# First layer's attention: the values of four key chunks at a time from group 3 on, with seven buffers for the weights

## Chip, cores and metric

One NeuronCore of a Trainium2 chip runs the whole program in one launch. The metric is the device time in microseconds (us) of that core; it is given as the median of several executions.

## What is computed

Two layers over an input `x` of 2 batches x 128 positions x 256 features. The change lies in the first step of the first layer, a cross attention with 16 heads of 16 features over 2048 keys per batch, in which keys and values are both the context:

```python
scores = jnp.einsum('bhqd,bhkd->bhqk', qh, kh) / math.sqrt(hd)
qi = jnp.arange(Sq)[:, None] + (Sk - Sq)
ki = jnp.arange(Sk)[None, :]
causal = ki <= qi
scores = jnp.where(causal[None, None], scores, jnp.asarray(MASKED_BIAS, scores.dtype))
attn = jax.nn.softmax(scores, axis=-1)
out = jnp.einsum('bhqk,bhkd->bhqd', attn, vh)
...
x = x + _L0_xattn_ref(_layernorm(x, axis=-1), ctx_2048, ctx_2048)
x = x + _L0_attn_ref(_layernorm(x, axis=-1), L0_attn_A_log, L0_attn_D, L0_attn_W_xproj)
x = x + _L0_ffn_ref(...)
```

The second step, `_L0_attn_ref`, is a state space scan: step sizes from a projection and a softplus, a decay `exp(dt * A)` and an input `dt * B * x` for each of 16 states, a scan over the 128 positions, and a sum over the states with `C`. After it come a low-rank mixture of experts, and in the second layer another cross attention, a local attention and a feed-forward mixture. Those later parts are not touched.

## The kernel before

Every engine has its own instruction list, written out by hand in Python loops; engines meet only through counting semaphores, and each list is carried out in order.

**Groups.** The 2 x 16 heads are cut into eight groups of four heads, `g` = 0 to 7 (four of batch 0, then four of batch 1). A group goes over its 2048 keys in 16 chunks of 128, `c` = 0 to 15; the text numbers chunks through as n = 16 g + c. Keys are stored as bfloat16 parts in `kS[g % 3]`.

**Three streams on TensorE.** For group g the loop (L1047 on) goes over pairs of chunks, k = 0 to 7, c = 2 k:

- `scores_shifted(g, c)` (L889, with a masking matmul L888 in the last chunk): four matmuls of one chunk's scores with the maxima subtracted, into one of two PSUM banks `score_b[n % 2]`. It waits for the exponential of chunk n - 2 (`exp_done`).
- `values(g, c)` (L902): four products with the values, 128x32 tiles in float32, two passes each, so 8 matmul records a chunk; `pv_done` counts chunks. In the pair k the chunks c - 2 and c - 1 are taken.
- `scores_for_max` (L858, with L860 to L862 where the mask lies): sixteen parts a group, which give the scores of the *next* group for its row maxima; `MAX_AT` sets how many follow each pair. Two parts fill one of two double banks; VectorE reduces it (L1647, piece 0 to 7). `max_to_rows(g + 1)` (L872) closes the group and waits for that group's maxima (`nm_done`, L1653 to L1658 on VectorE).

At k = 1 `outputs_to_rows(g - 1)` (L910, L911) transposes the finished group.

**ScalarE** takes the exponential of each chunk (L665) from `score_b` into a weight buffer `pT[n % 3]`, after waiting for the values of chunk n - 3. Between exponentials it does the steps of its `beside` table, keyed (group, chunk): the copy of the outputs (L644 at c = 2, L655 at c = 4), the softplus (L585, L588, at (5, 0) and (5, 1), the second with a load of another activation table), the decay's exponentials `decay_exp` (L600, at (6, 2) and (6, 6)) and sixteen copies `bc_copy` (L595).

**The scan of batch 0 runs in the same stretch.** After group 3 VectorE normalises batch 0 (L1390 to L1396, after piece 2 of group 5) and gives the layer norm; TensorE projects (L921, L930); VectorE makes the input (`step_and_input`, L1406, L1408) and splits the projected maps (`split_maps`, L1418 to L1422). TensorE then spreads 32 rows of B and C over the partitions in 16 steps, `spread` (L945) at `SPREAD_AT`, each of which waits for the copy of the step before. GpSimd makes the decay's exponents (L422, twice) and the inputs (L414, twice), VectorE scans (L1439, after piece 3 of group 7) and multiplies by C (`read_states`, L1445, after piece 6 of group 7, once all sixteen copies are there). GpSimd's list has, after the copy of group 6's values (L433), `decay_exponent(0)`, `decay_exponent(1)` and `state_input(0, 0)`, then the copy of group 7's values and `state_input(0, 1)`. The decay lies where the key parts of batch 1 lay, so its exponents wait until the keys of group 7 have been fetched as well as for `dtx_done`; the inputs wait for eight of the sixteen copies:

```python
pool.wait_ge(S("kS_in1"), 16 * REP * 3)
...
pool.wait_ge(S("bc_sb"), (8, 20)[b])
```

**SyncE** fetches keys and values. For group g from 3 on:

```python
sp.wait_ge(S("pv_done"), NCH * (g - 2))
values_in(g - 1)
```

followed by twelve transfers into `kS[g % 3]` (L287). For group 7 that is a wait for the values of chunk 79, the last of group 4.

## Time and profile before

| | |
|---|---|
| median of 3 runs | 515.19 us (515.15 to 516.58) |
| profiled execution, its own time | 514.26 us |
| its span | 512.0 us, 8986 instructions |
| PE (TensorE) busy | 425.1 us, 83% |
| weight loads busy | 311.0 us, 61% |
| DVE (VectorE) busy | 345.8 us, 68% |
| ACT (ScalarE) busy | 269.4 us, 53% |
| POOL (GpSimd) busy | 121.7 us, 24% |
| chain that ended last, by engine | PE 58%, DVE 23%, ACT 8%, issue 6% |
| L902, values of the chunks | 1024 matmuls, 45.9 us |
| L889, shifted scores | 512 matmuls, 51.0 us |
| L1439, scan | 12.0 us for the two of batch 0 |

The span is the time between the first and the last instruction in the records; the execution's own time is 2.3 us more. Busy times of engines overlap, so they don't add up to the span, and matmuls are pipelined: a record starts when the matmul enters and ends when its last result is out, so several are open at once. The eight groups take the span from 38 us to 198 us.

### The profile page before, as it was taken

The page shows a single profiled execution, that of the slowest core. Times are in us where ns is not written, and L with a number is a line of the kernel's source. Part 1 is how long each engine was busy: PE and PEld are TensorE (multiplying, and loading weights), DVE is VectorE, ACT ScalarE, POOL GpSimd, SP SyncE. Part 2 cuts the span into 40 slices and gives each one's busy share as a digit, 9 for nine tenths or more (in the row PEclk, how much of TensorE's full clock was granted, in tenths as well). Part 3 has the DMA queues.
Part 4 walks back from the last instruction along what each step waited for, and adds up shares of the span by engine and source line. Part 5 has one row for each costly group of instructions (what it writes and reads, how often), then busy time and mean ns, then how long its engine had stood idle before and what let it go on. Part 6 is the DMA issues. An engine that isn't in the chain of part 4 may idle for free.

```text
span 512.0 us, 8986 instructions
## 1 busy us (share of the span) xinstructions
PE 425.1 (83%) x3584; PEld 311.0 (61%) x3584; DVE 345.8 (68%) x544; ACT 269.4 (53%) x579; POOL 121.7 (24%) x78
## 2 busy tenths in 40 slices
PE   0269889988875985694989998997789799999997
PEld 0116556656553773534843473445679699999996
DVE  3797667676569935699565565684562589778772
ACT  4305697766585452540322442457784076777762
POOL 3010545000274000280003235250300213333300
PEclk9999899998797798678999999999799979999999
DMA  6598176652511082000920000005800197540000
GB/s 217 141 291 214 28 187 166 165 133 52 150 48 32 3 299 68 25 0 1 397 97 1 1 0 3 0 0 193 300 1 2 43 360 246 173 165 1 2 2 20
DMA packets 24329, 54.11 MB, mean 106 GB/s; under 512 B 5113, under 2 KB 13529, under 8 KB 20954
## 3 DMA queue, kind: packets, MB, share of 16 engines
q1 hardware_dynamic: 24288, 53.54, 33.4%
q8 instruction: 28, 0.46, 0.4%
q14 instruction: 13, 0.11, 0.1%
HBM read 40.65 MB, written 0.26 MB: 80 GB/s over the span
## 4 chain that ended last, share of the span: by engine, by line
PE 58%; DVE 23%; ACT 8%; issue 6%; DMA 2%; POOL 2%; SPq 0%; ACTq 0%; DVEq 0%; POOLq 0%
PE ps L1268 17%; PE ps L1089 8%; PE ps L902 5%; PE ps L889 4%; PE ps L858 4%; DVE mx L1647 4%; DVE reg_b L1439 3%; DVE reg_a L1439 2%; ACT reg_b L665 2%; PE ps L1233 2%; PE ps L1223 2%; PE ps L1222 2%; PE ps L997 2%; PE ps L1016 1%; DVE reg_b L1430 1%
## 5 line engine op out<-in xcount | busy, mean ns | idle before, releaser
L1647 DVE TENSOR_REDUCE mx<-ps 128x1 f32<-128x1024 f32 x64 | 77.0, 1221 | 40.4 <-PE ps L858 28.3
L665 ACT ACTIVATE reg_b<-ps 128x512 f32<-128x512 f32 x128 | 75.4, 599 | 39.9 <-PE ps L889 20.8
L889 PE MATMUL ps<-qreg,reg_b 98*128 98x128 bf16 x512 | 51.0, 235 | 6.1 <-ACT reg_b L665 4.7
L889 PEld LDWEIGHTS ps<-qreg,reg_b 98*128 98x128 bf16 x512 | 38.3, 106 | 18.6 <-ACT reg_b L665 8.8
L1268 PE MATMUL ps<-part_a 128*128 128x256 f32 x384 | 48.2, 283 | 0.4 <-DVE part_a L1792 0.4
L386 POOL TENSOR_TENSOR rstd<-ve,cf 128x1 f32<-128x1 f32 x12 | 6.8, 563 | 172.3 <-DVE ve L1341 172.3
L858 PE MATMUL ps<-reg_b,qreg 96*128 96x512 bf16 x96 | 36.3, 448 | 13.7 <-DMA reg_b<-reg_b 7.6
L1089 PE MATMUL ps<-reg_b,xT 128*128 128x512 f32 x96 | 47.6, 618 | 0.0
L1268 PEld LDWEIGHTS ps<-part_a 128*128 128x128 f32 x384 | 46.9, 192 | 0.6 <-DVE part_a L1792 0.6
L902 PE MATMUL ps<-reg_b 128*32 128x128 f32 x1024 | 45.9, 299 | 0.0
L800 ACT ACTIVATE reg_a<-ps,b 128x256 f32<-128x256 f32 x64 | 30.2, 472 | 24.0 <-PE ps L1268 24.0
L1792 DVE TENSOR_TENSOR part_a<-reg_a,part_a 128x256 fp32r<-128x256 f32 x64 | 26.1, 431 | 18.8 <-ACT part_a L803 18.8
L1268 PE MATMUL ps<-part_a,part_b 128*128 128x256 f32 x288 | 38.2, 293 | 0.6 <-DVE part_a L1792 0.6
L1268 PEld LDWEIGHTS ps<-part_a,part_b 128*128 128x128 f32 x288 | 37.1, 202 | 0.9 <-DVE part_a L1792 0.8
L674 ACT COPY reg_a<-ps 128x512 f32<-128x512 f32 x24 | 14.0, 587 | 44.7 <-PE ps L1089 44.7
L902 PEld LDWEIGHTS ps<-reg_b 128*32 128x32 f32 x1024 | 26.8, 117 | 7.3 <-issue 1.9
L498 POOL CAST part_b<-reg_b 128x1024 fp32r<-128x1024 f32 (+1 forms) x9 | 16.3, 1827 | 46.6 <-PE ps L1268 34.0
L803 ACT CAST part_a<-reg_a 128x256 fp32r<-128x256 f32 x64 | 26.0, 407 | 2.0
L1089 PEld LDWEIGHTS ps<-reg_b,xT 128*128 128x128 f32 x96 | 16.3, 189 | 16.7 <-issue 16.7
L858 PEld LDWEIGHTS ps<-reg_b,qreg 96*128 96x128 bf16 x96 | 8.2, 103 | 26.4 <-DVE mx L1647 12.0
L460 POOL TENSOR_TENSOR qreg<-qreg,cf 128x16 f32<-128x16 f32 x4 | 13.4, 3356 | 35.2 <-DVE qreg L1587 35.2
L1739 DVE TENSOR_TENSOR part_a<-reg_b,part_a 128x1024 fp32r<-128x1024 f32 (+1 forms) x12 | 20.8, 1744 | 0.8 <-ACT part_a L811 0.8
(279 smaller groups left out, 869.8 us busy)
## 6 DMA issues: line engine op xcount, KB each, us to landing
reg_b<-in_w SPq DMA_DIRECT2D x16, 512.0 KB, 7.1
reg_b<-in_w SPq DMA_DIRECT2D x8, 1024.0 KB, 7.0
reg_b<-reg_b SPq DMA_DIRECT2D x56, 128.0 KB, 3.7
reg_b<-in_w_qkv SPq DMA_DIRECT2D x3, 2048.0 KB, 13.4
reg_b<-reg_a SPq DMA_DIRECT2D x40, 128.0 KB, 3.6
reg_a<-in_ctxK SPq DMA_DIRECT2D x4, 1024.0 KB, 6.9
reg_a<-in_ctx SPq DMA_DIRECT2D x8, 512.0 KB, 5.1
reg_a<-in_ctxT SPq DMA_DIRECT2D x2, 2048.0 KB, 9.7
```

The costliest lines, as they stand in the source:

```text
L665: sc.activation(pT[n % 3], score_b[n % 2], ACT.Exp).then_inc(S("exp_done"), 1)
L800: sc.activation(hid[layer][:, m, :], ps[:, 2 + m, 0:NB * P], ACT.Gelu, bias=(b1, b2)[layer][:, e, m:m + 1]).then_inc(S(f"h{layer + 1}_sb"), 1)
L803: sc.copy(hid_high[layer][:, m, :], hid[layer][:, m, :]).then_inc(S(f"h{layer + 1}_high"), 1)
L858: mm = pe.matmul(score_a[m % 2][:, i, :], q, k, start=True, stop=True)
L889: mm = pe.matmul(cols, kS[g % 3][0:SROWS, c // 8, j, P * (c % 8):P * (c % 8 + 1)], qT[b][0:SROWS, HPG * hg + j, :], start=not last, stop=True)
L902: mm = pe.matmul(ps[VW * j:VW * (j + 1), 7, 0:P], va[g % 2][:, c, j, :], pT[n % 3][:, P * j:P * (j + 1)], start=c == 0, stop=c == NCH - 1)
L1089: mm = pe.matmul(bank(b, n % 2), xT[b][:, i, :], w_qkv[:, j, i, 512 * n:512 * (n + 1)], start=False, stop=i == KD - 1)
L1268: mm = pe.matmul(out, left[u], right[v], start=(i, u, v) == (0, 0, 0), stop=(i, u, v) == (len(terms) - 1, 0, 1))
L1439: link(ve.tensor_tensor_scan(state[b][:, h].rearrange("p n l -> p (n l)"), decay[b][:, h].rearrange("p n l -> p (n l)"), state[b][:, h].re ...
L1647: ve.reduce_max(mx[:, piece // 2, piece % 2:piece % 2 + 1], score_a[m % 2].rearrange("p i k -> p (i k)"), X_AXIS).then_inc(S("max_done"), 1)
L1739: ve.tensor_tensor(low[e % 2][i], raw[e % RAW][i], high[e % 2][i], ALU.subtract).then_inc(S("w_low"), 1)
L1792: ve.tensor_tensor(hid_low[layer][:, m, :], hid[layer][:, m, :], hid_high[layer][:, m, :], ALU.subtract).then_inc(S(f"h{layer + 1}_low"), 1)
```

## The change

From group 3 on (`QUADS = 3`) TensorE no longer takes the values of two chunks in every pair, but of four in every second one: at odd k the chunks n - 6 to n - 3 of the pair that begins with chunk n. Seven weight buffers instead of three make room for it (four more at `reg_b` 16384 to 17920), and ScalarE waits for the values of chunk n - 7. The outputs of the group before are transposed at k = 2 instead of k = 1, and ScalarE copies them at c = 4 and c = 6 instead of 2 and 4. `state_maps` moves from (5, 4) to (5, 7), the sixteen spreads move to other chunks, and on VectorE `split_maps` comes after `step_and_input` and one more piece.

```diff
-SPREAD_AT = [(5, c) for c in range(8, 15)] + [(6, c) for c in (0, 1, *range(4, 11))]
+SPREAD_AT = [(5, c) for c in range(9, 15)] + [(6, c) for c in (0, 1, 2, *range(7, 14))]
+QUADS = 3
...
-        pT = [reg_b[:, 24576 + 512 * i:24576 + 512 * (i + 1)] for i in range(3)]
+        pT = [reg_b[:, a:a + 512] for a in (24576, 25088, 25600, 16384, 16896, 17408, 17920)]
+
+        def weight_buffer(n):
+
+            first = NCH * QUADS
+            return pT[n % 3] if n < first else pT[(n - first + 3) % 7]
...
-                    if g >= 1 and c == 2:
+                    if g >= 1 and c == (2 if g < QUADS else 4):
                         unnormalised(g - 1)
-                    if g >= 1 and c == 4:
+                    if g >= 1 and c == (4 if g < QUADS else 6):
                         sc.wait_ge(S("oT_ready"), g)
...
-                    if n >= 3:
+                    if 3 <= n < NCH * QUADS:
                         sc.wait_ge(S("pv_done"), n - 2)
-                    sc.activation(pT[n % 3], score_b[n % 2], ACT.Exp).then_inc(S("exp_done"), 1)
+                    elif n >= NCH * QUADS + 4:
+                        sc.wait_ge(S("pv_done"), max(n - 6, NCH * QUADS))
+                    sc.activation(weight_buffer(n), score_b[n % 2], ACT.Exp).then_inc(S("exp_done"), 1)
...
-                      (5, 4): [(misc_read, "o_all", 5), (state_maps, 0)], (6, 4): [(misc_read, "o_all", 6)],
+                      (5, 7): [(misc_read, "o_all", 5), (state_maps, 0)], (6, 7): [(misc_read, "o_all", 6)],
...
+            def chunks_at(g, k):
+
+                n = NCH * g + 2 * k
+                if g < QUADS:
+                    return range(max(n - 2, 0), n)
+                if k % 2 == 0:
+                    return ()
+                return range(max(n - 6, NCH * QUADS - 2), n - 2)
...
-                    if k > 0:
-                        values(g, c - 2)
-                        values(g, c - 1)
-                    elif g > 0:
-                        values(g - 1, NCH - 2)
-                        values(g - 1, NCH - 1)
-                    if k == 1 and g >= 1:
+                    for chunk in chunks_at(g, k):
+                        values(*divmod(chunk, NCH))
+                    if k == (1 if g < QUADS else 2) and g >= 1:
...
-            values(NG - 1, NCH - 2)
-            values(NG - 1, NCH - 1)
+            for c in range(NCH - 4, NCH):
+                values(NG - 1, c)
...
-                      (5, 4): [(ln_apply, 1, 0)], (5, 8): [(step_magnitude, 0)], (6, 2): [(split_maps, 0)],
-                      (6, 3): [(step_and_input, 0)], (7, 3): [(scan, 0, 0)], (7, 6): [(read_states, 0, 0)]}
+                      (5, 4): [(ln_apply, 1, 0)], (5, 8): [(step_magnitude, 0)], (6, 3): [(step_and_input, 0)],
+                      (6, 4): [(split_maps, 0)], (7, 3): [(scan, 0, 0)], (7, 6): [(read_states, 0, 0)]}
```

How the lists now stand, at three places. (Line numbers of the changed kernel are larger: L897 is the old L889, L910 the old L902, L866 the old L858; on ScalarE L673 is the old L665, L601 the old L595, L606 the old L600.)

TensorE at the start of group 5, from the scores of chunks 80 and 81 to those of chunk 83 and the values behind them. `exp_done` is ScalarE's count of exponentials, `max_done` VectorE's of reduced pieces. Before:

```order
L889 MATMUL ps<-qreg,reg_b 128x128 [waits exp_done,ones_in,nm_rows]
L889 MATMUL ps<-qreg,reg_b 128x128 x3
L889 MATMUL ps<-qreg,reg_b 128x128 [waits exp_done]
L889 MATMUL ps<-qreg,reg_b 128x128 x3
L902 MATMUL ps<-reg_b 32x128 [waits exp_done]
L902 MATMUL ps<-reg_b 32x128 x3
L902 MATMUL ps<-reg_b 32x128 [waits exp_done]
L902 MATMUL ps<-reg_b 32x128 x3
L858 MATMUL ps<-reg_b,qreg 128x512 [waits max_done]
```

Now:

```order
L897 MATMUL ps<-qreg,reg_b 128x128 [waits exp_done,ones_in,nm_rows]
L897 MATMUL ps<-qreg,reg_b 128x128 x3
L897 MATMUL ps<-qreg,reg_b 128x128 [waits exp_done]
L897 MATMUL ps<-qreg,reg_b 128x128 x3
L866 MATMUL ps<-reg_b,qreg 128x512 [waits max_done]
L868 MATMUL ps<-reg_b,qreg 128x384
L869 MATMUL ps<-reg_b,qreg 128x128
L870 MATMUL ps<-cb 128x128
L897 MATMUL ps<-qreg,reg_b 128x128 [waits exp_done]
L897 MATMUL ps<-qreg,reg_b 128x128 x3
L897 MATMUL ps<-qreg,reg_b 128x128 [waits exp_done]
L897 MATMUL ps<-qreg,reg_b 128x128 x3
```

Right behind the last of these stand the values of chunks 76 to 79. The values of chunks 78 and 79 stood behind the scores of chunk 81; they now stand behind the scores of chunk 83.

ScalarE at the start of group 6, from the maxima's rows to the second copy after them; L595 is a copy of spread rows, L600 the exponential of the decay. Before:

```order
L571 COPY qreg<-ps 2x512
L665 ACTIVATE reg_b<-ps 128x512 x2
L595 COPY reg_b<-ps 128x256
L665 ACTIVATE reg_b<-ps 128x512
L644 COPY o_sb<-ps 128x128
L600 ACTIVATE reg_a<-reg_a 128x2048
```

Now:

```order
L577 COPY qreg<-ps 2x512
L673 ACTIVATE reg_b<-ps 128x512 x2
L601 COPY reg_b<-ps 128x256
L673 ACTIVATE reg_b<-ps 128x512
L606 ACTIVATE reg_a<-reg_a 128x2048
L601 COPY reg_b<-ps 128x256
```

The copy ahead of the decay's exponential was the eighth of the sixteen and is now the seventh; the eighth follows the exponential.

ScalarE at the end of group 6, the last copy and what follows it up to the next group's rows. Before:

```order
L665 ACTIVATE reg_b<-ps 128x512
L595 COPY reg_b<-ps 128x256
L665 ACTIVATE reg_b<-ps 128x512 x4
L571 COPY qreg<-ps 2x512
L665 ACTIVATE reg_b<-ps 128x512 x3
```

Now:

```order
L673 ACTIVATE reg_b<-ps 128x512
L601 COPY reg_b<-ps 128x256
L673 ACTIVATE reg_b<-ps 128x512
L577 COPY qreg<-ps 2x512
L673 ACTIVATE reg_b<-ps 128x512 x5
```

The sixteenth copy stood ahead of chunk 11's exponential and now stands ahead of chunk 14's.

## Rows read from the trace of the kernel before

**Rows 1.** Groups 3 and 6: us; busy PE, PEld, DVE, ACT, POOL; clock; DMA share, GB/s.
```profile
91.20:105.70 14.50, 14.01 (x229) 9.50 (x228) 10.34 (x12) 10.70 (x21) 1.04 (x1) 1.00 0.57 147
...
148.30:174.40 26.10, 19.46 (x244) 12.73 (x242) 22.19 (x19) 16.25 (x31) 10.09 (x3) 0.74 0.15 39
```

**Rows 2.** Timeline of TensorE, group 3: start us, us, engine, line, operation.
```profile
95.28 0.61 PE L889 MATMUL ps<-qreg,reg_b 98*128 98x128 bf16 x8
95.82 0.64 PE L902 MATMUL ps<-reg_b 128*32 128x128 f32 x16
96.40 0.34 PE L860 MATMUL ps<-reg_b,qreg 96*128 96x384 bf16 x1
```

**Rows 3.** One line's own view, L902: ns of one, min/median/max.
```profile
L902 PE MATMUL ps<-reg_b x1024: 269/273/423, 40.9 to 197.4; 128*32 128x128 f32 x171
```

**Rows 4.** Timeline of all engines, chunks 80 to 84: bracket is idle before, releaser.
```profile
126.11 0.33 SPq L261 DMA_DIRECT2D reg_a<-in_ctx  x1
...
127.71 1.28 ACT L665 ACT_TABLE_LOAD   x1
129.00 0.60 ACT L665 ACTIVATE reg_b<-ps 128x512 f32<-128x512 f32 x1
...
129.65 0.61 PE L889 MATMUL ps<-qreg,reg_b 98*128 98x128 bf16 x4 [2.78 <-ACT reg_b L665]
130.19 1.08 PE L902 MATMUL ps<-reg_b 128*32 128x128 f32 x16
```

**Rows 5.** The same timeline, SyncE's last two transfers of group 7's keys.
```profile
133.36 1.22 SPq L287 DMA_DIRECT2D reg_b<-reg_b  x2
```

**Rows 6.** DMA issues, 126 to 140 us: median us to landing of those two.
```profile
reg_b<-reg_b SPq DMA_DIRECT2D x2, 128.0 KB, 3.2
```

**Rows 7.** Timeline, 138 to 172 us: GpSimd's exponents and VectorE's maxima.
```profile
139.10 7.17 POOL L422 TENSOR_TENSOR reg_a<-tmpb,ea 128x2048 f32<-128x2048 f32 x2 [5.65 <-DVE tmp L1408]
...
144.36 1.94 DVE L1653 TENSOR_TENSOR m<-mx 128x4 f32<-128x4 f32 x1
...
147.07 0.33 PE L872 MATMUL ps<-cb,nm 128*2 128x128 bf16 x3 [0.62 <-ACT reg_b L595]
...
171.49 0.16 DVE L1653 TENSOR_TENSOR m<-mx 128x4 f32<-128x4 f32 x1
```

**Rows 8.** Timeline, 149 to 173 us: inputs, decay and the two scans.
```profile
149.69 4.55 POOL L414 TENSOR_TENSOR reg_a<-tmp,reg_b 128x2048 f32<-128x2048 f32 x1 [3.41 <-ACT reg_b L595]
...
150.26 1.92 ACT L600 ACTIVATE reg_a<-reg_a 128x2048 f32<-128x2048 f32 x1
...
154.28 1.04 POOL L433 COPY reg_b<-reg_a 128x1024 f32<-128x1024 f32 x1
...
155.28 4.54 POOL L414 TENSOR_TENSOR reg_a<-tmp,reg_b 128x2048 f32<-128x2048 f32 x1
...
156.55 7.55 DVE L1439 TENSOR_TENSOR_SCAN reg_a<-reg_a 128x2048 f32<-128x2048 f32 x1
...
172.80 4.42 DVE L1439 TENSOR_TENSOR_SCAN reg_a<-reg_a 128x2048 f32<-128x2048 f32 x1
```

**Rows 9.** Timeline, 214 to 234 us: VectorE and GpSimd side by side, batch 1.
```profile
215.50 8.82 DVE L1430 TENSOR_TENSOR reg_b<-tmpb,ea 128x2048 f32<-128x2048 f32 x2
215.60 13.11 POOL L414 TENSOR_TENSOR reg_b<-tmp,reg_b 128x2048 f32<-128x2048 f32 x2 [0.46 <-ACT reg_b L595]
```

**Rows 10.** Timeline after the first scan: spreads, copies, values and C.
```profile
165.42 1.04 PE L858 MATMUL ps<-reg_b,qreg 96*128 96x512 bf16 x2 [3.14 <-DVE mx L1647]
...
167.95 1.08 PE L902 MATMUL ps<-reg_b 128*32 128x128 f32 x16
168.03 2.29 DVE L1445 TENSOR_TENSOR reg_a<-reg_a,reg_b 128x2048 f32<-128x2048 f32 x1 [0.32 <-ACT reg_b L595]
```

**Rows 11.** Chain that ended last, in order of time: start us, us, what.
```profile
177.26 2.30 DVE reg_a L1445
...
189.48 0.44 PE ps L824 x2
```

More of the change, by code:

```diff
@@ L901, in values @@
                 for j in range(HPG):
-                    mm = pe.matmul(ps[VW * j:VW * (j + 1), 7, 0:P], va[g % 2][:, c, j, :], pT[n % 3][:, P * j:P * (j + 1)],
+                    mm = pe.matmul(ps[VW * j:VW * (j + 1), 7, 0:P], va[g % 2][:, c, j, :], weight_buffer(n)[:, P * j:P * (j + 1)],
                                    start=c == 0, stop=c == NCH - 1)
@@ L1031, in _ @@
                 beside.setdefault(at, []).append((spread, 0, i))
-            read_before_rows = {2: ("qT_sb", 4), 3: ("qT_sb", 6), 5: ("z_sb", 1), 6: ("bc_sb", 7), 7: ("bc_sb", 16)}
+            read_before_rows = {2: ("qT_sb", 4), 3: ("qT_sb", 6), 5: ("z_sb", 1), 6: ("bc_sb", 6), 7: ("bc_sb", 16)}
             read_before_outputs = {5: ("bc_sb", 9)}
```

## Prediction

> **What bounds the kernel now.** I began with the chain that ended last: it goes through the attention at every group, so what moves the end of group 7 moves the end of the program. Next the busy times by stretch [rows 1]. They show two kinds of group. In group 3 TensorE is busy 14.01 of 14.50 us: it is the bound. Group 6 lasts 26.10 us with TensorE busy 19.46, ScalarE 16.25 and VectorE 22.19, so there something else decides. The timeline says what: scores part 12 is held 3.14 us behind a VectorE reduction [rows 10], the reduction behind a scan of 7.55 us, and the scan had to wait for GpSimd's first input, which ends at 154.24 [rows 8]. From that scan on the chain stays on VectorE (three reductions, the product with C, one more reduction, the maxima, the second scan, the second product that ends at 179.56) and reaches the next layer norm's transposes at 189.48 [rows 11]. So two chains meet in groups 5 and 6, and the question is what the change does to the one through GpSimd and VectorE.
>
> **What is gained.** Eight matmuls of scores start at 95.28 and the values at 95.82 [rows 2]. One of these matmuls lasts 0.22, so the eight with 0.61 are (0.61 - 0.22) / 7 = 0.056 us apart and would need 0.45; 0.09 is extra. The sixteen of the values with 0.64, one of 0.27 [rows 3], are 0.025 apart and need 0.40, but the next matmul comes after 0.58: 0.18 extra. One batch of values costs 0.27 us for going over to the narrow tiles and back. From group 3 to the end there are 41 batches, and afterwards 21: 20 x 0.27 = 5.4 us of TensorE's time, the most that the edit can take away.
>
> **Why little of it arrives.** In a pair without values TensorE needs 8 x 0.056 = 0.45 plus two or three parts of 0.22: about 1 us. ScalarE needs 2 x 0.60 [rows 4] for the pair, about 1.3 with its waits, and with only two score banks the second scores of the next pair wait for it: 0.3 to 0.5 us in each double pair, against the 0.27 saved. Extra weight buffers don't help; they relieve the values, not the banks. Outputs of a group are copied two chunks later, so normalising batch 0 starts about 1 us later. I put groups 3 and 4 at 0 to +1 us, and take +0.5.
>
> **First cost: group 7's keys are fetched later.** SyncE sends them off once chunk 79's values are done, at 126.11 [rows 4]. The order above puts these values behind the scores of chunk 83, which wait for chunk 81's exponential. That stands behind the softplus with two loads of a table, the one listed of 1.28 us and its like before it; it ends at 129.60, and TensorE goes on at 129.65 after 2.78 us of idling. Then 0.54 of scores, and four chunks of values where the rows have two for 130.19 to 131.21, at half clock: 2.04 instead of 1.02. That is 132.2, with the 0.5 from above 132.7, call it +6.6. The transfers keep their 10.9 us (last one issued at 133.97 [rows 5], 3.2 to landing [rows 6], so 137.2): 143.8. GpSimd's exponents, which began at 139.10 when VectorE had their input [rows 7], had 1.9 us to spare; now the keys come last, and the two run 143.8 to 151.0: **+4.7 us**.
>
> **Second cost: the maxima of group 6 fall into them.** VectorE's first small operation at 144.36 took 1.94 us and ended with GpSimd's at 146.3; the same one takes 0.16 with GpSimd idle [rows 7]. Four such follow each other, and the last has two SBUF inputs like the first. In the new order they come at about 146 (the split and the input in the other order cost nothing, the third piece comes at the same time), in the middle of 143.8 to 151.0. The first gets in between the two exponents at best, the last then waits for the end of the second: maxima at about 151.4, rows at 151.5 instead of 147.07, **+4.4 us**. TensorE stands still about 3 us for it, and I expect its clock at the lower of its two levels (1.2 instead of 2.4 GHz) afterwards, as after the 2.78 us before 129.65, where sixteen matmuls of values took 1.08 instead of 0.64 [rows 2, 4]. The Trainium skill's page "SBUF — State Buffer", section "SBUF: two separate sides", says that a GpSimd instruction and a VectorE one with two SBUF inputs or in a two-port mode lock each other out for the whole instruction. By that rule the maxima end as I have them; were the port shared by bandwidth, they would end 3 us earlier.
>
> **Third cost: the eighth copy.** From the rows to GpSimd's first input it took 149.69 - 147.07 = 2.6 us. Added ahead of the eighth copy: the decay's exponential, 1.92 [rows 8]; one more chunk with its spread and copy, about 0.8 (165.42 to 167.95 holds two parts of 0.4 and two such rounds [rows 10]); two more chunks of values, 0.4; and at the lower clock about 0.6 more. 6.3 us, so the input starts at 157.8 and ends at 162.35, +8.1.
>
> **What comes back.** The first scan takes 7.55 us, the second 4.42 [rows 8]: the first waited until 159.8 for GpSimd's second input. In batch 1 both engines took turns: two of VectorE in 8.82 and two of GpSimd in 13.11, about the sum of both alone, 4 x 2.3 and 4.5 [rows 9]. In the new order the scan waits behind the copy of the values (1.04) and then, if turns are taken, goes before the second input: 163.5 to 167.9. Before, it ended at 164.1: **+3.8 us** of the 8.1 is left.
>
> **Fourth cost: the sixteenth copy.** The product with C waits for it: 168.03 - 164.10 = 3.9 us after the scan [rows 10]. TensorE is again held at part 12 until 1.3 us after the scan, and from there now has two parts, a spread round and scores (the 2.5 of the same rows), four chunks of values at low clock (2.1), two parts (0.9), then two chunks each with a spread that waits for the copy before (2 x 0.9), and ScalarE the exponential of chunk 13 and the copy (1.0). 1.3 + 2.5 + 2.1 + 0.9 + 1.8 + 1.0 = 9.6 at the low clock, 7.5 at the high one. I take 9.0: **+5.1 us**. The last piece, the maxima, the second scan all stand behind that product.
>
> **Sum.** 3.8 + 5.1 = 8.9, and about 0.3 in group 7, where the scores of the last chunks wait for exponentials: **+9.2 us**. VectorE's chain from the product with C to 189.48 is unchanged, and after group 7 nothing is. The profiled execution's own 514.26 becomes 523.5; the median of the runs is 0.9 above it, so I say **524.4 us**. The sum's own bounds are +5.5 (high clock throughout, two of the 3 us of collision spared) and +13.5 (the scan loses the turn and waits for the second input too, 4.5 us).
>
> **Rivals.**
>
> - *No late exponents.* If the values of chunk 79 are not held up that much, or GpSimd's exponents slip past the maxima, the first two costs shrink to about 1 us. For it: 1.9 us to spare. Against: the table loads are in the way whatever else changes. Then the input starts 4 us late, the scan at 159.4 once the values are copied and ends at 163.8, -0.3; the sixteenth copy still costs 3.6 to 5.1. Sum +4.5: **519.7 us**. Chance 0.22.
> - *Faster.* The saved switches arrive: TensorE reaches chunk 13 of group 6 so early that the sixteenth copy is no later than 3.9 us after the scan. This decides at 3.9 us against the 7.5 that I work out, so the spreads would have to be done before the scan, which the hold at part 12 prevents; it needs the scan itself held up less by GpSimd than I think. Price: 2.7 (half of 5.4) to 5.4 off, say **511.5 us**. Chance 0.12.
> - *Nothing moves.* Gain in groups 3 and 4 of up to 2 us against a short delay: 515, chance 0.05.
> - That the change doesn't halve the batches can be left out: the order shows them in fours.
> - *More than the sum.* Scan behind the second input and low clock: 528, taken into the main case's range.
>
> **How the numbers follow.** Main case 0.61, no late exponents 0.22, faster 0.12, nothing 0.05. A measurement of this kernel can tell about 0.3%, 1.5 us, from no change. So slower 0.83, same 0.05, faster 0.12. The range takes the main case and the first rival with their bounds, 517 to 529, and leaves out the two cases below and a little above.
>
> **What would show it.** Right, step by step: idle time of TensorE before chunk 83's scores; group 7's first transfer issued at 132 to 134; GpSimd's exponents starting at about 144 released by a transfer, not by VectorE; one of VectorE's four-column operations lasting over 1 us; TensorE's rows for group 6 at 151 or later; a first scan of about 5 us instead of 7.55; VectorE idle for over 3 us before the product with C, released by a copy. Wrong: a first transfer before 129, exponents starting by 140, or that product starting within 4 us of the scan.

## The result: slower by 3.4%, and the profile after

| | before | after |
|---|---|---|
| median | 515.17 us of 4 runs (513.49 to 516.58) | 529.50 us of 4 runs (528.03 to 530.94) |
| ratio, 95% interval | | 1.034 (1.029 to 1.039) |
| profiled execution, own time | 514.26 us | 530.94 us |
| span | 512.0 us | 528.8 us |

The ratio is the one on record, from fast executions of both kernels; the two medians above are 2.8% apart. The forecast was 524.4 us with a range of 517 to 529; the kernel took 529.5, half a microsecond outside. The sign and most steps of the mechanism were as forecast; the size was not, 14.3 us instead of 9.2, and one step, the start of the scan, was worked out wrongly.

From the page of the profile after, its span and its line on busy time:

```profile
span 528.8 us, 8982 instructions
...
PE 428.9 (81%) x3584; PEld 316.2 (60%) x3584; DVE 347.1 (66%) x544; ACT 267.8 (51%) x579; POOL 125.7 (24%) x78
```

No engine works much more than before (TensorE 428.9 us against 425.1, GpSimd 125.7 against 121.7). The 16.8 us of span are waits for the most part, and some low clock. To find them I measure one stretch in every kernel, from group 3's first scores to the end of group 7's last values. Busy times by stretch, before (columns as in [rows 1]); the windows are group 3, group 5 up to group 6's rows, and from there to the product with C:

```profile
91.20:105.60 14.40, 13.91 (x228) 9.46 (x227) 10.34 (x12) 10.60 (x21) 1.04 (x1) 1.00 0.57 148
...
124.60:147.00 22.40, 17.70 (x224) 11.67 (x222) 14.71 (x21) 14.99 (x29) 8.21 (x3) 0.85 0.37 95
147.00:168.00 21.00, 14.51 (x193) 9.38 (x197) 16.07 (x9) 14.06 (x26) 10.09 (x3) 0.81 0.19 48
```

After, cut at the same events:

```profile
92.40:106.80 14.40, 13.19 (x213) 9.20 (x212) 10.33 (x12) 10.51 (x21) 1.04 (x1) 1.00 0.55 148
...
127.00:152.50 25.50, 15.09 (x208) 10.46 (x207) 18.14 (x21) 14.07 (x27) 8.21 (x3) 0.86 0.33 84
152.50:181.50 29.00, 21.68 (x245) 14.88 (x245) 13.70 (x10) 16.10 (x31) 14.14 (x3) 0.71 0.14 34
```

Group 3 lasts 14.40 us in both, group 4 is 1.2 us longer (20.20 against 19.00, the gap between the first windows), group 5 3.1 (25.50 against 22.40), and the third window 8.0 (29.00 against 21.00), at a lower clock; the rest of the stretch, 30.6 after and 29.6 before, gives 1.0. The stretch is 106.4 us before and 119.7 after, **+13.3**. Of the other 3.5 us, 1.2 lie before group 3, where nothing was changed, and 2.3 after group 7. The second figure has no link to an edit: over all fourteen profiled kernels what follows group 7 took from 310.5 to 316.7 us, at random as far as I can see, and single executions of the kernel before took 509.0 to 517.2. So below, the stretch tells where time goes, and the ratio what it is worth.

### The profile page after: what moved, and what is told of

Same layout as the page of the kernel before. It is cut to its first block, busy times and chain, and to the rows that moved or that the text cites. A ratio compares the mean times of both kernels' runs of the same rounds, so it can differ in the third digit from the quotient of the medians.

```text
span 528.8 us, 8982 instructions
## 1 busy us (share of the span) xinstructions
PE 428.9 (81%) x3584; PEld 316.2 (60%) x3584; DVE 347.1 (66%) x544; ACT 267.8 (51%) x579; POOL 125.7 (24%) x78
## 4 chain that ended last, share of the span: by engine, by line
PE 59%; DVE 22%; ACT 8%; issue 7%; DMA 2%; POOL 1%; SPq 0%; ACTq 0%; DVEq 0%; POOLq 0%
PE ps L1281 17%; PE ps L1102 8%; PE ps L910 7%; PE ps L866 4%; PE ps L897 4%; DVE mx L1660 3%; DVE reg_b L1452 2%; ACT reg_b L673 2%; PE ps L1246 2%; DVE reg_a L1452 2%; PE ps L1235 1%; PE ps L1236 1%; PE ps L1005 1%; PE ps L1024 1%; DVE reg_b L1443 1%
## 5 line engine op out<-in xcount | busy, mean ns | idle before, releaser
L1660 DVE TENSOR_REDUCE mx<-ps 128x1 f32<-128x1024 f32 x64 | 76.8, 1221 | 47.2 <-PE ps L866 35.6
L673 ACT ACTIVATE reg_b<-ps 128x512 f32<-128x512 f32 x128 | 74.4, 598 | 42.1 <-PE ps L897 32.9
L897 PE MATMUL ps<-qreg,reg_b 98*128 98x128 bf16 x512 | 50.1, 234 | 7.7 <-ACT reg_b L673 6.6
L897 PEld LDWEIGHTS ps<-qreg,reg_b 98*128 98x128 bf16 x512 | 38.3, 106 | 20.3 <-ACT reg_b L673 10.4
L866 PE MATMUL ps<-reg_b,qreg 96*128 96x512 bf16 x96 | 37.3, 461 | 16.0 <-DVE mx L1660 8.2
L1102 PE MATMUL ps<-reg_b,xT 128*128 128x512 f32 x96 | 50.2, 647 | 0.0
L1281 PE MATMUL ps<-part_a 128*128 128x256 f32 x384 | 48.2, 283 | 0.4 <-DVE part_a L1805 0.4
L910 PE MATMUL ps<-reg_b 128*32 128x128 f32 x1024 | 44.7, 313 | 0.0
L1805 DVE TENSOR_TENSOR part_a<-reg_a,part_a 128x256 fp32r<-128x256 f32 x64 | 26.2, 435 | 18.3 <-ACT part_a L811 18.3
L910 PEld LDWEIGHTS ps<-reg_b 128*32 128x32 f32 x1024 | 30.5, 124 | 5.5 <-issue 1.5
L504 POOL CAST part_b<-reg_b 128x1024 fp32r<-128x1024 f32 (+1 forms) x9 | 16.5, 1847 | 47.9 <-PE ps L1281 34.0
L866 PEld LDWEIGHTS ps<-reg_b,qreg 96*128 96x128 bf16 x96 | 7.6, 103 | 29.9 <-DVE mx L1660 13.7
L439 POOL COPY reg_b<-reg_a 128x1024 f32<-128x1024 f32 x8 | 8.3, 1047 | 54.8 <-DMA reg_a<-in_ctx 33.1
## 6 DMA issues: line engine op xcount, KB each, us to landing
reg_b<-in_w SPq DMA_DIRECT2D x16, 512.0 KB, 7.5
reg_a<-in_ctx SPq DMA_DIRECT2D x8, 512.0 KB, 4.6
```

What stands on the lines that cost most here:

```text
L504: pool.tensor_copy(high[e % 2][i], raw[e % RAW][i]).then_inc(S(name), 1)
L673: sc.activation(weight_buffer(n), score_b[n % 2], ACT.Exp).then_inc(S("exp_done"), 1)
L866: mm = pe.matmul(score_a[m % 2][:, i, :], q, k, start=True, stop=True)
L897: mm = pe.matmul(cols, kS[g % 3][0:SROWS, c // 8, j, P * (c % 8):P * (c % 8 + 1)], qT[b][0:SROWS, HPG * hg + j, :], start=not last, stop=True)
L910: mm = pe.matmul(ps[VW * j:VW * (j + 1), 7, 0:P], va[g % 2][:, c, j, :], weight_buffer(n)[:, P * j:P * (j + 1)], start=c == 0, stop=c == N ...
L1102: mm = pe.matmul(bank(b, n % 2), xT[b][:, i, :], w_qkv[:, j, i, 512 * n:512 * (n + 1)], start=False, stop=i == KD - 1)
```

## The steps in the trace after

The timeline of all engines where chunk 79's values were forecast to be late; start us, us, engine, line, operation, in brackets the idle time before and its releaser:

```profile
129.80 1.28 ACT L673 ACT_TABLE_LOAD   x1
131.09 1.08 ACT L673 ACTIVATE reg_b<-ps 128x512 f32<-128x512 f32 x2
131.75 0.61 PE L897 MATMUL ps<-qreg,reg_b 98*128 98x128 bf16 x4 [3.24 <-ACT reg_b L673]
132.29 1.94 PE L910 MATMUL ps<-reg_b 128*32 128x128 f32 x32
134.28 0.33 SPq L267 DMA_DIRECT2D reg_a<-in_ctx  x1
```

TensorE idles 3.24 us before chunk 83's scores, the four chunks of values follow at the low clock, and SyncE's transfers for group 7 begin at 134.28 (the one listed is group 6's values, the keys follow). What that does to GpSimd's exponents and VectorE's maxima, and those to TensorE's rows for group 6:

```profile
144.73 7.17 POOL L428 TENSOR_TENSOR reg_a<-tmpb,ea 128x2048 f32<-128x2048 f32 x2 [4.73 <-DMA reg_b<-reg_b]
...
146.15 2.21 DVE L1666 TENSOR_TENSOR m<-mx 128x4 f32<-128x4 f32 x1
...
148.39 3.54 DVE L1668 TENSOR_SCALAR negm<-m,cf 128x4 f32<-128x4 f32 x1
...
151.96 0.17 DVE L1670 CAST nm<-negm 128x4 bf16<-128x4 f32 x1
...
152.44 0.48 PE L880 MATMUL ps<-cb,nm 128*2 128x128 bf16 x3 [4.53 <-issue]
```

The exponents are now released by a transfer. VectorE's first small operation ends at 148.36 with the first exponent, the second at 151.93 with the second. Then the first input, the scan and what holds it:

```profile
157.24 1.92 ACT L606 ACTIVATE reg_a<-reg_a 128x2048 f32<-128x2048 f32 x1
159.03 0.38 ACT L601 COPY reg_b<-ps 128x256 f32<-128x256 f32 x1
...
159.56 4.53 POOL L420 TENSOR_TENSOR reg_a<-tmp,reg_b 128x2048 f32<-128x2048 f32 x1 [7.66 <-ACT reg_b L601]
...
160.29 1.94 PE L910 MATMUL ps<-reg_b 128*32 128x128 f32 x32
...
162.28 0.33 SPq L267 DMA_DIRECT2D reg_a<-in_ctx  x1
...
165.44 0.62 PE L866 MATMUL ps<-reg_b,qreg 96*128 96x512 bf16 x1
...
165.68 1.22 DVE L1660 TENSOR_REDUCE mx<-ps 128x1 f32<-128x1024 f32 x1 [1.23 <-PE ps L870]
...
166.91 1.04 POOL L439 COPY reg_b<-reg_a 128x1024 f32<-128x1024 f32 x1 [2.82 <-DMA reg_a<-in_ctx]
166.98 5.25 DVE L1452 TENSOR_TENSOR_SCAN reg_a<-reg_a 128x2048 f32<-128x2048 f32 x1
167.91 8.62 POOL L420 TENSOR_TENSOR reg_a<-tmp,reg_b 128x2048 f32<-128x2048 f32 x1
```

The decay's exponential and then the eighth copy stand ahead of the input, as in the forecast. The input ends at 164.09, but the scan starts at 166.98: it stands in VectorE's list behind the reduction of piece 3, which waits until 165.68 for its parts. It stood behind that reduction in the kernel before as well, 2.3 us after the end of the input (154.24):

```profile
155.25 1.22 DVE L1647 TENSOR_REDUCE mx<-ps 128x1 f32<-128x1024 f32 x1 [0.51 <-PE ps L862]
```

One thing is new. SyncE fetches group 7's values (L267) only once the values of chunk 95 are done, and these are now in a batch of four one pair later: the transfer goes off at 162.28, 2.7 us after the first input has started, where before it went 0.1 us after it (149.77 against 149.69), and GpSimd's copy waits for it until 166.91. Before, the copy came right behind the first input, and the second input began 1.3 us ahead of the scan [rows 8]; now the scan is first.

And the product with C:

```profile
181.06 0.37 ACT L601 COPY reg_b<-ps 128x256 f32<-128x256 f32 x1
181.46 2.29 DVE L1458 TENSOR_TENSOR reg_a<-reg_a,reg_b 128x2048 f32<-128x2048 f32 x1 [5.62 <-ACT reg_b L601]
```

VectorE idles 5.62 us for the sixteenth copy, where it idled 0.32 [rows 10].

TensorE's clock in successive windows of this stretch (columns as in [rows 1]):

```profile
148.80:155.70 6.90, 3.27 (x41) 2.27 (x42) 3.46 (x3) 1.17 (x2) 3.10 (x1) 0.51 0.00 0
155.70:159.10 3.40, 1.59 (x20) 1.09 (x18) 2.36 (x2) 3.10 (x5) 0.00 (x0) 1.00 0.00 0
159.10:165.90 6.80, 6.34 (x57) 4.36 (x58) 1.44 (x2) 3.87 (x10) 4.53 (x1) 0.50 0.35 80
165.90:172.70 6.80, 3.26 (x58) 2.33 (x56) 6.73 (x4) 4.00 (x7) 5.79 (x2) 1.00 0.23 67
```

The clock goes back and forth between 2.4 GHz (1.00) and 1.2 GHz (0.50). It falls for the second time at 159.10, after TensorE has been busy 1.59 of 3.40 us, and this low window, in which it is busy 6.34 of 6.80 us, lies exactly on the work that the scan waits for.

## The experiments

Twelve more kernels were run. All times below but the ratio are of one profiled execution each, in us after the first scores of group 3 (stretch: end of group 7's last values). The ratio is the one on record, to the kernel before on the same chip, with its 95% interval; it can differ from the quotient of two medians by a few tenths of a per cent.

| kernel | GpSimd's exponents begin | rows of group 6 | first input | scan | product with C | rows of group 7 | stretch | ratio |
|---|---|---|---|---|---|---|---|---|
| before | 47.9 | 55.8 | 58.4 | 65.3 to 72.9 | 76.8 | 82.0 | 106.4 | 1 |
| after | 52.4 | 60.1 | 67.2 | 74.6 to 79.9 | 89.1 | 93.5 | 119.7 | 1.034 (1.029 to 1.039) |
| a1 | 48.3 | 64.4 | 70.7 | 75.3 to 79.8 | 88.7 | 93.1 | 119.4 | 1.030 (1.022 to 1.038) |
| a2 | 52.5 | 60.2 | 67.5 | 73.8 to 78.2 | 87.5 | 87.7 | 118.7 | 1.023 (1.012 to 1.033) |
| a3 | 52.3 | 60.3 | 66.1 | 71.4 to 75.9 | 84.7 | 89.1 | 115.4 | 1.017 (1.009 to 1.026) |
| b1 | 48.2 | 56.2 | 61.7 | 68.1 to 76.0 | 85.3 | 89.7 | 116.0 | 1.017 (1.009 to 1.025) |
| c1 | 49.8 | 58.6 | 64.2 | 70.4 to 74.9 | 84.1 | 88.5 | 115.7 | 1.019 (1.014 to 1.024) |
| c2 | 52.3 | 60.0 | 67.1 | 74.6 to 79.8 | 84.7 | 89.7 | 115.0 | 1.011 (1.004 to 1.017) |
| c3 | 48.9 | 58.8 | 62.7 | 68.0 to 72.4 | 77.3 | 82.5 | 107.7 | 1.001 (0.997 to 1.004) |
| d1 | 46.4 | 62.7 | 68.4 | 74.9 to 82.7 | 92.1 | 96.5 | 122.0 | 1.024 (1.019 to 1.029) |
| e1 | 47.7 | 55.7 | 58.3 | 65.2 to 69.6 | 74.3 | 79.8 | 105.3 | 1.000 (0.996 to 1.004) |
| e2 | 54.7 | 55.5 | 61.8 | 66.5 to 70.9 | 79.6 | 83.9 | 113.5 | 1.014 (1.006 to 1.022) |
| e3 | 49.7 | 58.5 | 62.4 | 67.7 to 72.1 | 81.5 | 81.6 | 112.1 | 1.016 (1.011 to 1.022) |
| e4 | 48.7 | 56.6 | 59.3 | 66.1 to 70.6 | 78.7 | 79.6 | 108.0 | 1.001 (0.998 to 1.005) |

**a1, the late values put back.** On the kernel after:

```diff
                 n = NCH * g + 2 * k
+                if g == 5 and k < 2:
+                    return range(n - 4, n) if k == 0 else ()
```

> The changed kernel, but the values of chunks 76 to 79 stand in pair 0 of group 5 and none in pair 1, so that the fetch of group 7's keys no longer stands behind the table loads. Theory (late keys, then GpSimd's exponents across the maxima): the first key transfer starts at about 128 us instead of 134.7, the exponents at about 140 released by VectorE's input or nearly so, no small VectorE operation is held, the rows of group 6 come 4 to 5 us earlier, and the time falls from 529.5 by about 5, to 523 to 526. Rival (the quads themselves cost the time, by the two score banks): 529 to 530, no change.

The keys came early and the exponents began at 48.3, yet the stretch got hardly shorter (119.4), and the median was 527.75 us, not 523 to 526. Here is why, on the timeline of a1:

```profile
137.91 0.22 DVE L1437 CAST bc_split<-bc_res 32x128 bf16<-32x128 f32 x1
...
138.09 7.17 POOL L428 TENSOR_TENSOR reg_a<-tmpb,ea 128x2048 f32<-128x2048 f32 x2 [4.30 <-DMA reg_b<-reg_b]
...
138.48 3.30 DVE L1437 CAST bc_split<-bc_res 32x128 bf16<-32x128 f32 x1
...
141.82 3.59 DVE L1436 TENSOR_TENSOR bc_res<-bc_res,bc_split 32x128 f32<-32x128 f32 x1
...
145.72 0.39 PE L953 MATMUL ps<-bc_split,cb 96*128 96x128 bf16 x2 [7.69 <-DVE bc_split L1437]
```

The change also put the splitting of the maps behind the input. So with early keys the exponents fall on the split instead of on the maxima: two operations of 0.22 and 0.28 us alone take 3.30 and 3.59, and TensorE idles 7.69 us before the first spread. The late keys had kept the split clear. Undoing them by themselves moves the collision and takes nothing away.

**c1, the keys early again and the split ahead of the input.** a1's edit, and (the split at (6, 3); in the kernel before it stood at (6, 2))

```diff
-(6, 3): [(step_and_input, 0)], (6, 4): [(split_maps, 0)],
+(6, 3): [(split_maps, 0), (step_and_input, 0)],
```

> The changed kernel with the values of chunks 76 to 79 in pair 0 of group 5, and VectorE's split of the maps ahead of the scan's input again. Moving the values alone brought the keys back (exponents at 138.1) and left the rows at 154.2, since the split then fell into GpSimd's exponents. Theory (lock between GpSimd and VectorE, on the maxima or on the split, whichever is behind): with both out of its way the split ends before the exponents begin, the first copy of spread rows comes at about 140 instead of 142.6 or 146.5, the rows of group 6 at 148 to 149, and from the first scores of group 3 to the last values it takes 116 instead of 119.7 us. Rival (the rows of group 6 are late by TensorE's own order): rows at 152 or later, 119.

Neither collision is left: every operation of split and maxima takes 0.17 to 0.29 us. The stretch falls by 4.0 us against the kernel after. So the exponents' fall on VectorE's small operations costs some 4 us, on the maxima (after) as on the split (a1), and moving the keys alone doesn't get rid of it. The 4.0 may understate it: group 6's rows still come 2.7 us later than in the kernel before (58.6), since split and input now stand together ahead of a reduction, and TensorE idles 3.54 us behind the reductions that follow.

**d1, the orders of the change with the values in twos.** On the kernel after:

```diff
-QUADS = 3
+QUADS = 8
...
-            for c in range(NCH - 4, NCH):
+            for c in range(NCH - 2, NCH):
```

> The changed kernel with the values in twos in all groups and three buffers; state maps, split and spreads stay at the changed kernel's places. Theory (side work): close to the kernel before with the spreads moved (115.9 us from group 3's first scores to the last values, 1.017 of the time before), so 116 to 118, and the quads make the other 2 to 4. Rival (the quads are all of it): 107 and 515.

The stretch is 122.0, 2.3 longer than with fours. The same collision as in a1 is there (casts of 2.18 and 3.21 us, first spread after 6.04 us of idling):

```profile
142.53 3.21 DVE L1435 CAST bc_split<-bc_res 32x128 bf16<-32x128 f32 x1
...
146.36 0.40 PE L953 MATMUL ps<-bc_split,cb 96*128 96x128 bf16 x2 [6.04 <-DVE bc_split L1435]
```

So the orders that came with the fours cost this much without them. The forecast of 116 to 118 was too low: it left out the collision, and the scan takes 7.8 us again. That the fours themselves cost nothing can't be read from this, as d1's collision and scan are other ones than those of the kernel after.

**e2, the exponents held until the maxima are through.** On the kernel after:

```diff
                 if g == 6:
+                    pool.wait_ge(S("nm_done"), 7)
                     decay_exponent(0)
```

> The changed kernel, with one wait more: GpSimd's exponents of the decay wait for the maxima of group 6. Theory (of the second cost: the maxima are held by the exponents): no small operation of VectorE is held, the rows of group 6 come 55 to 56 us after group 3's first scores instead of 60.1, the first input at 63 instead of 67.2, and the last values at 116 instead of 119.7. Rival (rows late by TensorE): rows at 59 or later.

```profile
144.02 0.16 DVE L1667 TENSOR_TENSOR m<-mx 128x4 f32<-128x4 f32 x1
...
144.68 0.17 DVE L1672 TENSOR_TENSOR nm<-negm,nm 128x4 bf16<-128x4 f32 x1
...
144.93 7.17 POOL L428 TENSOR_TENSOR reg_a<-tmpb,ea 128x2048 f32<-128x2048 f32 x2 [6.98 <-DVE nm L1672]
```

An added wait makes the kernel faster. The exponents start 2.3 us later, the four small operations are short, group 6's rows come at 55.5 instead of 60.1, and the stretch is 6.2 us shorter. This takes away the second cost alone, and one wait is enough for it. At the rows it is worth 4.6 us, as forecast; at the scan's start the gain is 8.1, and of that 6.2 reach the end.

**a3, copies ahead of whatever else ScalarE has beside a chunk.** On the kernel after; it puts the eighth copy ahead of the decay's exponential:

```diff
-                beside.setdefault((g, c + 1), []).append((bc_copy, 0, i))
+                beside.setdefault((g, c + 1), []).insert(0, (bc_copy, 0, i))
```

> The changed kernel, but ScalarE makes the eighth copy of spread rows ahead of the decay's exponential (1.92 us) at chunk 2 of group 6. Theory (the copy is held by the exponential, and with it GpSimd's input, the spread behind it and the values of chunks 92 to 95): the input starts 1.9 us earlier, the scan by about 2, the time falls by 2 to 527.5. Rival (other work hides it): 529 to 530.

The first input starts only 1.1 us earlier, but the scan 3.2 and the product 4.4, and the stretch is 4.3 shorter. The timeline of a3:

```profile
157.25 1.91 ACT L606 ACTIVATE reg_a<-reg_a 128x2048 f32<-128x2048 f32 x1
...
157.50 4.54 POOL L420 TENSOR_TENSOR reg_a<-tmp,reg_b 128x2048 f32<-128x2048 f32 x1 [6.60 <-ACT reg_b L601]
...
157.92 1.08 PE L910 MATMUL ps<-reg_b 128*32 128x128 f32 x32
...
161.52 1.23 DVE L1660 TENSOR_REDUCE mx<-ps 128x1 f32<-128x1024 f32 x1 [0.71 <-PE ps L870]
...
162.82 4.42 DVE L1452 TENSOR_TENSOR_SCAN reg_a<-reg_a 128x2048 f32<-128x2048 f32 x1
163.97 4.10 POOL L439 COPY reg_b<-reg_a 128x1024 f32<-128x1024 f32 x1 [1.93 <-DMA reg_a<-in_ctx]
```

Exponential and input now run together, the same 32 matmuls of values take 1.08 us instead of 1.94, and piece 3 is reduced 5.2 us after the input's start, instead of 7.3. Part of this is the clock; how much, no run separates. The last row shows the lock from the other side: GpSimd's copy, 1.04 us elsewhere, takes 4.10 under the scan.

**b1, the spreads alone, on the kernel before.**

```diff
-SPREAD_AT = [(5, c) for c in range(8, 15)] + [(6, c) for c in (0, 1, *range(4, 11))]
+SPREAD_AT = [(5, c) for c in range(9, 15)] + [(6, c) for c in (0, 1, 2, *range(7, 14))]
...
-6: ("bc_sb", 7)
+6: ("bc_sb", 6)
```

> The kernel before with one part of the change alone: the sixteen spreads at the changed kernel's places. Values stay in twos, buffers three. Theory (third and fourth cost are the spreads' places): the eighth copy comes after the decay's exponential and the sixteenth ahead of chunk 14's, the product with C starts 4 to 8 us later, time 519 to 523. Rival (the quads cost the time): 515 to 516.

```profile
150.98 4.52 POOL L414 TENSOR_TENSOR reg_a<-tmp,reg_b 128x2048 f32<-128x2048 f32 x1 [6.31 <-ACT reg_b L595]
...
157.40 7.86 DVE L1439 TENSOR_TENSOR_SCAN reg_a<-reg_a 128x2048 f32<-128x2048 f32 x1
...
174.61 2.29 DVE L1445 TENSOR_TENSOR reg_a<-reg_a,reg_b 128x2048 f32<-128x2048 f32 x1 [5.74 <-ACT reg_b L595]
```

The places of the sixteen spreads alone, with no fours and no late keys, cost 9.6 us of stretch and 1.7% of the time: 3.1 by the scan's end, where the eighth copy was late, and 5.4 more by the product, where the sixteenth was.

**c2, the last nine spreads drawn together.** On the kernel after; chunks 7, 8 and 9 take two each, so that the sixteenth is at chunk 10 again:

```diff
-SPREAD_AT = [(5, c) for c in range(9, 15)] + [(6, c) for c in (0, 1, 2, *range(7, 14))]
+SPREAD_AT = [(5, c) for c in range(9, 15)] + [(6, c) for c in (0, 1, 2, 7, 7, 8, 8, 9, 9, 10)]
```

> The changed kernel, but the spreads of group 6 behind chunk 2 stand two and two at chunks 7, 8 and 9 and one at 10, so that the sixteenth copy stands ahead of chunk 11's exponential as in the kernel before. Theory (the sixteenth copy holds VectorE): the product with C starts about 4 us after the first scan instead of 9.3, and from group 3's first scores to the last values it takes about 115 instead of 119.7 us. Rival (the copy is late because TensorE is, whatever its place): still over 8 us after the scan, 119.

```profile
164.66 5.27 DVE L1452 TENSOR_TENSOR_SCAN reg_a<-reg_a 128x2048 f32<-128x2048 f32 x1
...
174.78 2.29 DVE L1458 TENSOR_TENSOR reg_a<-reg_a,reg_b 128x2048 f32<-128x2048 f32 x1 [1.24 <-ACT reg_b L601]
```

Up to the scan's end nothing changes (79.8), then the product comes 4.9 us behind it instead of 9.2: -4.4, and -4.7 on the stretch. That is the fourth cost by itself.

**c3, four edits together and the fours kept.** c2, c1's two edits, and the eighth copy ahead of the decay's exponential:

```diff
+            beside[6, 2].insert(0, (bc_copy, 0, SPREAD_AT.index((6, 1))))
             for i, (g, c) in enumerate(SPREAD_AT):
+                if (g, c) != (6, 1):
```

> The changed kernel with all four: values of 76 to 79 earlier, split ahead of the input, eighth copy ahead of the decay's exponential, spreads in twos. The quads stay. Theory (the side work's places cost the time, the quads nothing): 105 to 108 us from group 3's first scores to the last values, against 106.4 in the kernel before, time 512 to 517, the kernel before within 1 %. Rival (the quads cost 4 us by the score banks): 110, time 519 to 521.

The stretch is 107.7 us, the ratio 1.001 (0.997 to 1.004) over ten runs: no difference from the kernel before. Of the 13.3 us 12.0 are gone, about the sum of what c1, c2 and a3 took away one by one (4.0 + 4.7 + 4.3 = 13.0). So the places of the side work account for nearly all of the loss.

What the fours are worth by themselves c3 doesn't tell, for it isn't the kernel before with fours put in. Its split stands at (6, 3) as in c1, and `state_maps` and the outputs' copies are where the change put them; group 6's rows come 3.0 us later than before. Against that its scan takes 4.42 us instead of 7.55, as the values' copy and the second input come late. Beside e1 below, which is the kernel before with a scan of 4.42, its stretch is 2.4 us longer.

**a2, e3: the product with C after the maxima of group 7.** In VectorE's list of the kernel after (a2) and of c3 (e3):

```diff
-(7, 6): [(read_states, 0, 0)]
+(7, 8): [(read_states, 0, 0)]
```

> The changed kernel, but VectorE's product with C stands behind the maxima of group 7 instead of ahead of their last piece. Theory (the sixteenth copy holds the maxima and with them group 7): rows of group 7 come 5 us or more earlier, the second scan still follows the product, the product itself stays bound by the copy at about 181; the time falls by 2 to 5. Rival (that copy costs nothing, VectorE's chain is the same in either order): 529 to 530.

> The kernel with quads and all four undone, and the product with C behind the maxima of group 7. In the changed kernel this brought the rows of group 7 forward by 5.8 us and the last values by 1.0. Theory (VectorE's chain through product, second scan and second product ends last, not TensorE's rows): rows of group 7 2 to 4 us earlier, last values within 1 us of 107.7. Rival (TensorE's group 7 ends last): last values 2 us or more earlier, 513 or less.

In a2 the rows of group 7 come 5.8 us earlier, the stretch is only 1.0 shorter: the chain of product, second scan and second product decides there, not the rows. For e3 I expected rows 2 to 4 us earlier and last values within 1 us of c3's, and both were wrong: the copy is hardly late in c3, so the product had only 1.2 us of waiting to give away. It moved 4.2 us back (81.5), the rows came 0.9 earlier, and the stretch is 4.4 longer.

**e1, e4: the lock in the kernel before.** GpSimd's second input waits for the piece of group 7 that follows the scan; e4 has the edit of a2 as well.

```diff
+                if (b, h) == (0, 1):
+                    pool.wait_ge(S("max_done"), 8 * 7 + 5)
                 pool.tensor_tensor(state[b][:, h], tmp[b][:, h * P:(h + 1) * P]
```

> The kernel before, with one wait more: GpSimd makes the second input only after the fifth piece of group 7 is reduced, so after the first scan. Theory (the scan's 7.55 us are 4.4 of its own and 3.1 of waiting for GpSimd's second input): the scan takes 4.4 us, the product with C starts about 3 us earlier, the second input still ends before the second scan needs it; 103 to 104 us from group 3's first scores to the last values instead of 106.4, and about 3 us less in all. Rival (the scan is slow for another reason, or the sixteenth copy holds the product anyway): 106, no change.

> The kernel before with both: second input after the first scan, product with C behind the maxima of group 7. Theory: like the second input alone, within 1 us, 103 to 104 us from group 3's first scores to the last values. Rival (TensorE's group 7 ends last): 2 us less than that.

```profile
155.11 4.42 DVE L1441 TENSOR_TENSOR_SCAN reg_a<-reg_a 128x2048 f32<-128x2048 f32 x1
...
160.97 4.53 POOL L416 TENSOR_TENSOR reg_a<-tmp,reg_b 128x2048 f32<-128x2048 f32 x1 [6.77 <-DVE mx L1649]
...
164.24 3.40 DVE L1447 TENSOR_TENSOR reg_a<-reg_a,reg_b 128x2048 f32<-128x2048 f32 x1
```

The scan takes 4.42 us instead of 7.55 [rows 8], so the 3.1 us were the wait for GpSimd's second input. The product starts 2.5 us earlier, then takes 3.40 instead of 2.29 since it meets the input that was moved; 1.1 us of stretch are left of the 2.4 to 3.4 expected, which the ratio of 1.000 (0.996 to 1.004) can't tell from none. e4, expected at 103 to 104, has 108.0, 1.6 us more than before, and a ratio of 1.001. No kernel of this study beats the one before by more than its measurement is uncertain.

## Why the prediction was wrong, and what in it was right

Each step in us, later than before, counted from group 3's first scores and taken from times to 0.01 us:

| step | forecast | measured |
|---|---|---|
| gain in groups 3 and 4 | +0.5 | 0 in group 3, +1.2 in group 4 |
| values of chunk 79 done | +6.6 | +7.0 |
| GpSimd's exponents | +4.7 | +4.5 |
| rows of group 6 | +4.4 | +4.2 |
| first input | +8.1 | +8.7 |
| end of the scan | +3.8 | **+7.0** |
| product with C | +8.9 | +12.3 |
| end of group 7 | +9.2 | +13.3 |

**Why little is gained.** As forecast, the saved switches don't arrive. The 32 matmuls of four chunks do take 1.08 us at the high clock where two batches of 16 took 2 x 0.64. TensorE's busy time of group 3 fell from 13.91 to 13.19 us, but in part because there is less in it: 213 matmuls instead of 228, since at its end the values of four chunks are still to come where there were two. It lasts 14.4 us all the same, in every kernel, and group 4 takes 20.2 to 21.5 us in the nine kernels with fours against 18.9 to 19.8 in the five with twos. The two score banks, my explanation, are at best one part of it by the trace: over groups 3 and 4 TensorE's waits for an exponential grew from 0.5 to 1.2 us, those for VectorE's reductions from 1.8 to 3.3. Neither was taken away in a run, so what holds the pace stays open.

**First and second cost** came as worked out, in place, size and releaser, a1 confirms the cause of the first (with chunk 79's values early the exponents begin at 48.3 instead of 52.4) and e2 that of the second: with the collision taken away and everything else in place 6.2 us of stretch go. By the rule of the Trainium skill, page "SBUF — State Buffer", section "SBUF: two separate sides", that the two engines hold the port for whole instructions, the second operation should end with the second exponent, and the trace agrees (151.93 and 151.90). I had it end there through the last of the four operations instead of the second, with the same sum. The step that I didn't work out is the split: I wrote that it and the input in the other order cost nothing. That holds only as long as the keys are late; a1 and d1 show 7 us of a held split when they are not. So "no late exponents", at 519.7 us the second likeliest case, was worked out wrongly in one of its two forms: a1 is the one with early values, and it took 527.75 us. The other, exponents that slip past the maxima, is e2, and its 519.0 us (a ratio of 1.014) is near. Two small slips of the working: the transfers' 10.9 us should read 11.1, with which the 143.8 comes out, and 9.2 and 4.5 make 13.7, not 13.5.

**The failed step is "What comes back".** It put the scan 1.1 us behind the end of the first input, held by GpSimd's copy of the values alone, so that of 8.1 us only 3.8 were left. In its place the runs show 7.0, and the 3.2 more fall into three: the input itself 0.6 later, the scan 2.9 behind its end instead of 1.1, and 5.25 us of scan where I had 4.42. The large one of these comes from VectorE's list, in which piece 3 of group 7 stands ahead of the scan. I had passed over that piece, though it held the scan in the kernel before too: it ended at 156.47, the scan began at 156.55, and the input had ended at 154.24. Now it ends at 166.90, since the same eighth copy that delays the input delays TensorE too: the ninth spread waits for it, and behind that stand three chunks' scores, four chunks of values in one batch (1.94 us at the low clock), the outputs' transposes and the parts of piece 3, the last of which ends at 165.64. a3 shows the link: with the copy first and the clock high, piece 3 is done 0.7 us after the input, and the scan ends at +3.0 and the stretch at +9.0. That these come near the forecast's 3.8 and 9.2 is partly chance, for a3 has one delay less than the kernel that was forecast.

**The turn of the scan was right by luck.** I had the scan stand behind the copy of the values and then go ahead of the second input. It did: it lost 0.83 us to the copy that began 0.07 ahead of it, and the second input, 4.53 alone, took 8.62. But the copy was to follow the first input at once. It came 2.82 us after it, since it waited for the transfer of group 7's values, which I hadn't looked at. At once behind the input it would have let the second input start at about 165.1, some 1.8 us ahead of the scan. With a lead of 1.0 to 1.3 us the second input went first in the kernel before, in b1 and in d1, and the scan took 7.55 to 7.86 us. In all nine kernels with fours the copy waits 1.5 to 2.9 us for that transfer, and in all nine the scan takes 4.42 to 5.27. By these rows the scan would have ended at about 165.1 + 4.5 + 4.4 = 174.0 instead of 172.2, an estimate: so the late values gave back some 1.8 us that the forecast had put down to turns. No run fetches them earlier to test it.

**Fourth cost.** The product came 9.2 us after the scan, forecast 9.0, and before 3.9. c2 takes 4.4 of it away.

**The remainder.** Group 7 from the rows on took 26.2 us against 24.3; of the wait from product to rows 0.9 went the other way: +1.0 together, forecast +0.3. Of the 14.3 us between the medians 1.0, and of the 16.8 between the profiled spans 3.5, lie outside the stretch and aren't explained; the kernel before varies by as much.

**Rivals.** "Faster" needed the product with C within 3.9 us of the scan, and it came at 9.2. "Nothing moves" is the time of c3, and it takes four edits and a shorter scan to get there. The rival "more than the sum", in which the scan waits for the second input too, gave nearly the right time (528) by a mechanism that the trace after doesn't have: the scan was held by VectorE's own piece 3, and the second input came behind it.

## What to carry to other kernels

A reordering that makes room for a saving on one engine has to be priced at every place it moves, and each item in a list twice: as what is released later, and as what stands ahead of somebody else's work (the eighth copy held the input and, through TensorE, the reduction ahead of the scan). Where two engines lock each other, undoing one delay may only move the collision to the next operation: try pairs of undone edits, and try adding a wait. When a term says that one instruction waits for another engine, check in the rows that it started when that engine was done; if not, what stands ahead of it in its own list may hold it. And a saving in an engine's busy time is none in the stretch if the engine then waits for the others, so look at the length of a stretch, and count the instructions in it before comparing busy times.

## What the runs showed that I had not expected

- The lock catches the smallest VectorE operations: a cast of 32x128 elements took 3.30 us instead of 0.22, one of 128x4 numbers with a scalar 3.54 instead of 0.23. A cast has a single SBUF input; the section of the Trainium skill named above counts, beside two inputs, a two-port mode, which this cast would have to be in. No run here tells which it is.
- It works in both directions and by turns: GpSimd's input took 8.62 us with a scan of 5.25 beside it, its copy 4.10 instead of 1.04 under a scan, and VectorE's scan 7.55 to 7.86 under an input, 4.42 alone.
- TensorE can lose its high clock in a stretch in which it is then nearly always busy (6.34 of 6.80 us at 0.50, from 159.10 on), and the same batch of values then takes 1.94 instead of 1.08 us.
- The 310 us behind the changed stretch differ by up to 6 us between the profiled executions, more than most edits here are worth.
